# A recurrence step moved inside the first-layer matmuls, its bias carried by the projections, and one more f16 half from ScalarE

## What is computed

```
xw = x @ Wx + b                              # all tokens at once
h_t = tanh(xw_t + h_{t-1} @ Wh)              # 128 steps, one after the other, 16 batches each
logits = h @ router_w.T ; top 2 of 8, softmax of the two
y_e = gelu(h @ w1_e.T + b1_e) @ w2_e.T + b2_e    # 8 experts, 512 hidden, gelu exact
x = x + sum over the top 2 of gate * y_e
```

## Time and profile before

| what | value |
|---|---|
| median of three timed runs | 316.67 us |
| the profiled execution, its own time | 315.6 us |
| its span from first to last instruction | 313.7 us |
| TensorE busy | 260.6 us, 83% of the span |
| VectorE busy | 268.7 us, 86% |
| ScalarE busy | 217.6 us, 69% |
| GpSimd busy | 86.2 us, 27% |
| mean granted TensorE clock | 0.924 |

### The profile page before, as it was taken

How to read it: one execution, slowest core, us unless ns; L and a number is a source line. 1 busy time by engine, 2 the same in 40 slices (tenths; PEclk the granted TensorE clock), 3 DMA queues, 4 the chain that set the end, 5 groups by cost and what they waited for, 6 DMA issues and landing times.

```text
span 313.7 us, 8438 instructions
## 1 busy us (share of the span) xinstructions
PE 260.6 (83%) x2611; PEld 192.6 (61%) x2611; DVE 268.7 (86%) x644; ACT 217.6 (69%) x436; POOL 86.2 (27%) x158
## 2 busy tenths in 40 slices
PE   5779750002869899999999999999999999999994
PEld 4624340000335687778788777777777777777873
DVE  4989899989897897879998889888789888799885
ACT  6368999991243777767766677767766666688882
POOL 2787999000019712101312112212110211101000
PEclk9959957555889999999999999999999999999999
DMA  6992553100004500000000000000000000001001
GB/s 188 326 285 49 101 101 67 33 0 0 0 0 65 104 3 0 0 3 2 18 0 2 0 2 25 4 0 0 0 2 19 16 0 0 2 3 34 0 2 27
DMA packets 28122, 11.67 MB, mean 37 GB/s; under 512 B 17449, under 2 KB 27074, under 8 KB 28098
## 3 DMA queue, kind: packets, MB, share of 16 engines
q1 hardware_dynamic: 27698, 11.16, 15.1%
q10 hardware_dynamic: 400, 0.20, 0.2%
HBM read 6.11 MB, written 1.05 MB: 23 GB/s over the span
## 4 chain that ended last, share of the span: by engine, by line
PE 72%; DVE 20%; issue 2%; DMA 2%; ACT 1%; POOL 0%; ACTq 0%; SPq 0%; DVEq 0%
PE bank L845 72%; DVE peak L592 6%; DVE big L688 3%; DVE big L698 2%; DVE peak L666 2%; DMA wn<-in_w_gate 2%; DVE big L704 1%; DVE big L671 1%; DVE big L706 1%; DMA y_sb<-in_cond 1%; DVE wyT L779 0%; DVE big L824 0%; DVE c L635 0%; DVE pkm L585 0%; ACT wyT L526 0%
## 5 line engine op out<-in xcount | busy, mean ns | idle before, releaser
L553 ACT ACTIVATE big<-bank,miscT 128x384 f32<-128x384 f32 (+2 forms) x160 | 96.2, 602 | 31.7 <-PE bank L845 28.1
L845 PEld LDWEIGHTS bank<-wt,big 128*128 128x128 f16 x1536 | 97.2, 98 | 29.0 <-issue 4.3
L845 PE MATMUL bank<-wt,big 128*128 (+1 forms) x1536 | 112.9, 219 | 1.8 <-DVE big L824 0.8
L824 DVE TENSOR_TENSOR big<-big 128x384 f16<-128x384 f32 (+2 forms) x160 | 94.3, 591 | 19.9 <-ACT big L555 15.6
L845 PE MATMUL bank<-big,wt 128*128 128x384 f16 (+2 forms) x480 | 108.7, 335 | 0.2 <-POOL big L375 0.2
L845 PEld LDWEIGHTS bank<-big,wt 128*128 (+1 forms) x480 | 46.0, 116 | 12.3 <-POOL big L375 0.3
L373 POOL CAST big<-q 128x64 f16<-128x64 f32 x32 | 13.5, 422 | 132.5 <-ACT q L543 132.3
L820 DVE CAST big<-big 128x512 f16<-128x512 f32 (+2 forms) x112 | 42.3, 378 | 7.8 <-ACT big L553 5.7
L543 ACT ACTIVATE q<-bank,miscT (+1 forms) x112 | 30.6, 274 | 23.2 <-PE bank L845 22.1
L845 PE MATMUL bank<-q,wxh 128*128 (+1 forms) x254 | 44.7, 252 | 2.2 <-ACT q L515 1.6
L845 PEld LDWEIGHTS bank<-q,wxh 128*128 128x128 f32 x254 | 39.1, 192 | 7.9 <-ACT q L515 3.8
(11 more groups left out here) (147 smaller groups left out, 295.8 us busy)
## 6 DMA issues: line engine op xcount, KB each, us to landing
wnat<-in_w SPq DMA_DIRECT2D x8, 512.0 KB, 7.6
x_sb<-in_x SPq DMA_DIRECT2D x4, 256.0 KB, 4.1
out_block<-wyT SPq DMA_DIRECT2D x16, 64.0 KB
wn<-in_w_gate ACTq DMA_DIRECT2D x1, 192.0 KB, 4.9
wn<-in_w_up SPq DMA_DIRECT2D x1, 192.0 KB, 5.3
wn<-in_w_down SPq DMA_DIRECT2D x1, 192.0 KB, 5.3
b_in<-in_b SPq DMA_DIRECT2D x12, 4.0 KB
wt<-wyT SPq DMA_TRANSPOSE x8, 3.0
```

What stands on the lines that cost most here:

```text
L553: A(g32[:, f, 0:w], ps_h[f][:, 0:w], ACT.Gelu, bias=bias, scale=1 / WS).then_inc(g32_done, 1)
L824: V.tensor_tensor(g_lo[:, par, f, 0:w], g32[:, f, 0:w], g_hi[:, par, f, 0:w], ALU.subtract).then_inc(g_lo_done, 1)
L845: return nc.tensor.matmul(o, l, r, start=start, stop=stop, skip_group_check=True)
```

## The change

It has four parts. The recurrence step is issued between the second and the third first-layer matmul of its slot rather than ahead of the three. The bias of the recurrence goes out of the tanh: it is loaded in two rows of a 33-row tile (rows 0 and 32), split in an f16 high and low row by GpSimd, and each `input_part` gets one more f16 matmul ahead of its three, with these rows as the stationary and a tile of ones as the moving operand. GpSimd gets two memsets and three small operations, SyncE one wait and two transfers of 0.5 KB. In chunk 1 the f16 high half of hidden block 3 is made by a second gelu on ScalarE instead of a cast on VectorE.

```diff
-HI_SCALAR = ((3,), (), (3,), (3,), (0, 1, 3))
+HI_SCALAR = ((3,), (3,), (3,), (3,), (0, 1, 3))
...
+            sp.wait_ge(bh_zeroed, 1)
+            for row in (0, BH_LO):
+                sp.dma_start(bh_in[row:row + 1, :], b_h.rearrange("(a n) -> a n", a=1)).then_inc(ld_bh, 16)
             sp.wait_ge(b2_zeroed, 1)
...
+            link(G.memset(ones[:, :], 1.0))
+            G.memset(bh_in[:, :], 0.0).then_inc(bh_zeroed, 1)
             G.memset(b2_in[:, :], 0.0).then_inc(b2_zeroed, 1)
...
+            pool.wait_ge(rw_done, 1)
+            pool.wait_ge(ld_bh, 32)
+            link(G.tensor_scalar(bh_in[:, :], bh_in[:, :], WS, 0.0, ALU.mult, ALU.add))
+            link(G.tensor_scalar(bh_rows[:, :], bh_in[:, :], 1.0, 0.0, ALU.mult, ALU.add))
+            low = slice(BH_LO, BH_LO + 1)
+            G.tensor_tensor(bh_rows[low, :], bh_in[low, :], bh_rows[low, :], ALU.subtract).then_inc(bh_ready, 1)
+            pool.wait_ge(bh_ready, 1)
             split_weights(2, 11)
...
-                A(h32[:, at], ps_rnn[:, at], ACT.Tanh, bias=bias_h, scale=1 / WS).then_inc(h32_done, 1)
+                A(h32[:, at], ps_rnn[:, at], ACT.Tanh, scale=1 / WS).then_inc(h32_done, 1)
...
-                          bias=bias_h, scale=1 / WS).then_inc(h32_done, 1)
+                          scale=1 / WS).then_inc(h32_done, 1)
...
-                mm3(ps_rnn[:, 0:B * (to - first)], wx_hi[:, :], wx_lo[:, :], x1_hi[:, at], x1_lo[:, at])
+                o = ps_rnn[:, 0:B * (to - first)]
+                mm(o, bh_rows[:, :], ones[:, 0:B * (to - first)], True)
+                mm3(o, wx_hi[:, :], wx_lo[:, :], x1_hi[:, at], x1_lo[:, at], False)
...
                     step = rnn_step(c, e2, s)
+                    if first and s == 0:
+                        pe.wait_ge(h_lo_done, START[c + 1] // (4 * B))
+
+                    t = slice(START[c], START[c + 1])
+                    o, w_hi, w_lo = ps_h[f][:, 0:WIDTHS[c]], *(wt_flat[:, w_cols(e2, s, 0, low)] for low in range(2))
+                    mm(o, w_hi, h_hi[:, t], True)
+                    mm(o, w_lo, h_hi[:, t], False)
                     if step is not None:
                         pe.wait_ge(h32_done, step)
                         mm(ps_rnn[:, bass.ds(rnn_column(c, step), B)], w_h32, h32[:, bass.ds((step - 1) * B, B)],
                            False).then_inc(rnn_mm, 1)
-                    if first and s == 0:
-                        pe.wait_ge(h_lo_done, START[c + 1] // (4 * B))
-
-                    t = slice(START[c], START[c + 1])
-                    mm3(ps_h[f][:, 0:WIDTHS[c]], wt_flat[:, w_cols(e2, s, 0, 0)], wt_flat[:, w_cols(e2, s, 0, 1)],
-                        h_hi[:, t], h_lo[:, t]).then_inc(hid_mm, 1)
+                    mm(o, w_hi, h_lo[:, t], False).then_inc(hid_mm, 1)
```

More of the change, by code:

```diff
@@ L49 @@
 W_CHUNKS = 2 * E
+BH_LO = 32
 SIG_V = 2
@@ L112, in program @@
         rw_lo = sb("rw_lo", [P, E], F16)
+        bh_in = sb("bh_in", [BH_LO + 1, P])
+        bh_rows = sb("bh_rows", [BH_LO + 1, P], F16)
+        ones = sb("ones", [BH_LO + 1, BANK], F16)
         b2_in = sb("b2_in", [3 * B2_ROWS, CT])
@@ L156, in program @@
             "hid_mm g32_done g_hi_done hi_v g_lo_done y_mm added b2_added stored")
+        bh_zeroed, ld_bh, bh_ready = sems("bh_zeroed ld_bh bh_ready")
         b2_zeroed, b2_ready, gate_split, gateT_mm, gateT_sb, b2_mm = sems(
@@ L508, in _ @@
             act.wait_ge(misc_sb, 1)
-            bias_h = miscT[:, SLOTS:SLOTS + 1]
             def first_step(r):
@@ L953, in _ @@
                     pe.wait_ge(small_w, 2)
+                    pe.wait_ge(bh_ready, 1)
                     pe.wait_ge(x1_lo_done, 1)
```

## The result

The changed kernel takes 312.43 us (median of four runs, 311.76 to 313.56) where the kernel before takes 316.8 (four runs, 316.2 to 317.63): a ratio of 0.987 with a 95% interval of 0.984 to 0.990, so 3.1 to 5.1 us faster. The forecast was 313.4. The two profiled executions, 315.6 and 312.67 us, differ by 2.9. Of all the runs in this document one, the profiled one of b2_later at 315.05 us, counts as slow and stays out of its ratio.

A forecast was written before the change was run, and what follows sets the result against it. TensorE was taken to bound the kernel from 136 us on, the recurrence chunk 0. Chunk 3 -1.15, chunk 2 -1.0, chunk 1 -0.2, chunk 0 -0.7, first steps -0.35, layer 0 +0.1 sum to -3.3: 313.4 us from 316.67, range 311.0 to 316.4.

The forecast's parts named there:

- The step's load hidden, 0.055 us a step: TensorE, chunks 1 to 3: a step behind a wide matmul hides its first weight load, saving 0.055 us each.
- Chunk 2, -1.0: Chunk 2: steps -1.8, bias matmul +0.22, stall at the chunk's end +0.35, loop's returns +0.25; together -1.0 us.
- Chunk 1, -0.2: Chunk 1: steps -1.1, bias matmul +0.22, chunk's end +0.25, loop's returns +0.45; together -0.2 us.
- Bias matmuls, 0.22, 0.22 and 0.16 on the path: Three of five added projection matmuls cost TensorE time: +0.22 in chunk 1, +0.22 in chunk 2, +0.16 in chunk 3.
- The added half, zero: Chunk 1: the extra gelu fits ScalarE and VectorE's relief shows nowhere; zero, bounds -0.3 and +0.5 us.
- Tanh 0.07 shorter, chunk 0 -0.7: ScalarE: each tanh loses 0.07 us without its bias; chunk 0, paced by the recurrence, gains 0.7 us in all.
- First steps, -0.35: Recurrence's first steps: some five of the last eight wait only for the step and gain from the shorter tanh, -0.35 us.
- Layer 0, +0.1, bounds 0 and +0.3: Layer 0: GpSimd's added operations cause one more collision with VectorE's product, +0.1 us, bounds 0 and +0.3.
- TensorE starves: Rival, chance 0.13: in looped slots of chunks 1 and 2 loads come too late to be hidden; 316.7 us, no change.
- slower: Rival, chance 0.10: a real stall in each looped step of chunks 0 to 2, 0.09 us each, +6 us: 319.4.
- More than forecast: Rival, chance 0.15: returns cost nothing, chunk 1 gets its full 0.055, chunk 0's long intervals shrink 0.1; -5.5, 311.2 us.
- One sign of being wrong: TensorE's granted clock falling after 106 us, where it was 1.00 throughout, would show the forecast wrong.

The follow-up runs named there:

- b2_later: states_first with chunk 1's added half back and GpSimd's second-layer bias split moved behind chunk 0's first three state splits; 312.0 us, ratio 0.987.
- step_only: The kernel before with only the step moved between the second and third first-layer matmul; 313.68 us against 316.06, ratio 0.993.
- step_first: The changed kernel with the step between the first and second first-layer matmul; 313.38 us, ratio 0.990 to the kernel before.
- no_hi: The changed kernel without chunk 1's added f16 half on ScalarE (a VectorE cast again); 313.53 us, ratio 0.992 to the kernel before.
- hi_only: The kernel before with only chunk 1's added f16 half on ScalarE; 316.85 us, ratio 1.003.
- bias_only: The kernel before with only the recurrence's bias moved from the tanh into the projections; 317.86 us, ratio 1.004.
- bias_late: The changed kernel with GpSimd's three bias-row operations behind its layer 0 weight halves; 312.88 us, ratio 0.989 to the kernel before.
- states_first: The changed kernel with the edits of step_first, no_hi and bias_late, and GpSimd splitting the first 16 states before its last weight half; 312.16 us, ratio 0.988.
- after_again: The changed kernel repeated without edit; 313.61 us against 315.84 for the kernel before, ratio 0.991.

## Why the prediction was right

- *The step's load hidden, 0.055 us a step.* Right: 0.056, in chunks 1, 2 and 3. It is shown by step_only, and by step_first, which keeps it at another place. Chunk 3 was forecast at -1.15 and measured -1.18. By the table's count its 24 steps are -1.34, and new gaps of 0.16 us in its loop take some back; the forecast's +0.16 for a bias matmul belonged to chunk 2 by that count, so the agreement of -1.15 and -1.18 is luck.
- *Chunk 2, -1.0.* Measured -1.18. Steps -1.79, end of chunk +0.34 (forecast +0.35), next bias matmul +0.27 (forecast 0.16). The +0.25 for the loop's returns was wrong there: no gap.
- *Chunk 1, -0.2.* The mis-sized term. Measured -0.84. I gave its looped slots 0.03 of the 0.055, as the recurrence needs 1.14 us a step; but the shorter tanh lowers that to 1.04, under the slot's 1.127, a link between two of my own terms that I did not draw. Even with the old tanh half was too little: step_only's steps take 0.14 in 30 of 32 cases, and only five slots are late. Steps -1.79, end +0.24, bias +0.32 (forecast 0.22), returns +0.39 (forecast +0.45, about right); these add up to -0.84.
- *Bias matmuls, 0.22, 0.22 and 0.16 on the path.* Too small by 0.1 each: 0.32, 0.32 and 0.27. I priced them by their columns alone, as first-layer matmuls in a row cost.
- *The added half, zero.* Wrong in its reason, inside its bounds. VectorE holds TensorE at one place of chunk 1 once slots are 1.127 us, 0.55 us in all (no_hi), and ScalarE's second gelu did hold the tanh while that was long (hi_only, 0.54 in all); I had argued from the old slots.
- *Tanh 0.07 shorter, chunk 0 -0.7.* The tanh lost 0.089, nearer to the pointer operand's price that I had set aside as a page's figure; the 0.078 between the two forms of the earlier trace rows, which I called a bound from above, was none. The short intervals are 1.04 apart (I had expected 1.07), the long ones of the round, 1.51 to 1.60, did not shrink. Chunk 0 as a whole came out at +0.1 in the first profile and at -0.35 where its clock was full throughout (no_hi; bias_only -0.4). By the table's count it holds a bias matmul of 0.32 that the forecast put in chunk 1; without it the two at full clock lost 0.67 and 0.72, the forecast's size. The rest up to +0.1 goes with the lower clock of 107.3 to 110.7 us: hi_only, whose chunk 0 is the old code, took 0.34 longer than before with the lower clock at 106.2 to 109.6.
- *First steps, -0.35.* Wrong: nothing. The stretch from the first step to the expert stage is 17.6 to 17.7 us in before, after, no_hi and bias_late alike (17.4 to 17.5 in hi_only and step_only, up to 18.0 in bias_only). GpSimd, nearly late before (a pause of 0.18 us ahead of its last split), is the bound; states_first, which relieves it, moves the stage by 2.3 us.
- *Layer 0, +0.1, bounds 0 and +0.3.* A collision of GpSimd with VectorE was the right thing to look for; the size was not: nothing in two profiles, about 1.7 us in three, and why the one or the other is open (bias_late).
- *Rivals.* "TensorE starves" and "slower" fell with the slots of 1.127 and 1.45 us, and the bias change did shorten the tanh. "More than forecast" came true in chunk 1 only. One sign of being wrong did come, a granted clock that falls after 106 us (0.57 from 107 to 111). It is no mark of the change as such: hi_only, without the moved step and the bias rows, has it at the same place, and no_hi and bias_late, with both, have not.

The total of -3.3 is thus near by luck as well: by the table's count chunk 1 was 0.6 too small a gain, chunk 0 (-0.5 with its bias matmul) and the first steps 0.5 to 1.0 too large, and the errors cancel. The profiled executions say -2.9, the timed medians -4.4 and -2.2. In the changed kernel's two profiles, 2.2 us apart, the difference lies ahead of chunk 1; that the timed runs differ for the same reason is likely, not shown.

## What to carry to other kernels

A small matmul whose weights take long to load belongs behind a wide one, and which wide one is chosen by what waits behind the small one's result: the earliest that still hides the load leaves most cover. Whether an engine is the bound of a stage is a statement about the stage's present period; when one edit shortens the period, judge the other edits against the new one. And a few small operations ahead of a long queue on GpSimd can be paid for on VectorE, where the two overlap; put them where GpSimd is idle and look at more than one profile.

## What the runs showed of the hardware

- Dropping the bias operand took an activation of 16 columns from 273 to 184 ns. The Trainium skill, ScalarE: Activation LUTs, under what a table load costs, says about 93 ns for each per-partition pointer operand; the trace agrees within 4 ns.
- An f32 step's two passes start 0.028 us apart behind a matmul of 384 or 512 columns and 0.084 behind one of 128, where the state is there in time.
- A VectorE product of 128x1024 took 1.23 us alone and up to 2.21 beside GpSimd (after_again), a subtraction of 128x256 1.26 us (states_first) where b2_later has 0.43.
- TensorE does not always have work queued: at the hardware loop's return 0.2 to 0.5 us pass in chunks 0 and 1. The queue of 64 entries that the Trainium skill gives (TensorE: Matmul & The Clock Gate, in its detail on the 32×32 sub-arrays) would not lead one to expect this; what the time is spent on was not measured.
- The same kernel meets the lower clock level at different places (107.3 to 110.7 us in one profile, 106.3 to 113.1 in another), each time after a stretch in which TensorE waited: 1.74 us for GpSimd in the one, 1.09 for VectorE in the other.
